# A context module with three recurrent scans: weights and images prepared differently, the image split moved into the scan's first blocks

## The reference

```
r, z = sigmoid(Wx_r x + Wh_r h), sigmoid(Wx_z x + Wh_z h)
n    = tanh(Wx_n x + r * (Wh_n h))
ctx  = (1 - z) * n + z * h
h    = tanh(conv1d(ctx, 3 taps) + bias)
```

## Time and profile before

| | before |
|---|---|
| median of 3 runs | 397.28 us |
| profiled execution, its own time | 396.7 us |
| its span | 395.0 us |
| PE / DVE / ACT / POOL busy | 323.7 / 316.5 / 273.0 / 16.6 us |
| mean granted TensorE clock | 0.969 |
| bytes read from HBM | 6.16 MB |

### The profile page before, as it was taken

One profiled execution on the slowest core, in us unless ns is written; L12 is line 12 of the kernel. 1 busy time (PEld: TensorE's weight loads), 2 busy tenths in 40 slices (PEclk: granted clock), 3 DMA queues, 4 the chain that ended last, 5 costly groups with the idle time before them and its releaser, 6 DMA issues.

```text
span 395.0 us, 7885 instructions
## 1 busy us (share of the span) xinstructions
PE 323.7 (82%) x2702; PEld 264.6 (67%) x2702; DVE 316.5 (80%) x750; ACT 273.0 (69%) x541; POOL 16.6 (4%) x26
## 2 busy tenths in 40 slices
PE   0101233487999999999999999999999999999995
PEld 0101112255888888888888888888888888885442
DVE  0663499969989989989989989889899899896532
ACT  6539896774777777777777777777777777775800
POOL 1072300000000000000000000000000000000000
PEclk9999968659999999999999999999999999999999
DMA  8700000000000000000000000000000000000544
GB/s 309 315 0 0 1 0 1 0 2 0 2 0 0 0 0 0 0 0 0 0 0 0 0 0 0 0 0 0 0 0 0 0 0 0 0 0 0 161 123 143
DMA packets 10199, 10.43 MB, mean 26 GB/s; under 512 B 465, under 2 KB 8785, under 8 KB 10193
## 3 DMA queue, kind: packets, MB, share of 16 engines
q1 hardware_dynamic: 10192, 10.36, 7.7%
HBM read 6.16 MB, written 4.19 MB: 26 GB/s over the span
## 4 chain that ended last, share of the span: by engine, by line
PE 76%; DVE 9%; ACT 7%; issue 3%; POOL 2%; DMA 1%; POOLq 0%
PE rz_bank L679 20%; PE conv_bank L679 15%; PE rz_bank L682 10%; PE n_bank L679 10%; PE conv_bank L682 8%; PE n_bank L682 5%; DVE x_rows L533 5%; ACT x_rows L371 2%; DVE x_rows L525 2%; PE rz_bank L766 1%; PE n_bank L770 1%; PE rz_bank L770 1%; PE n_bank L768 1%; PE rz_bank L768 1%; PE n_bank L766 1%
## 5 line engine op out<-in xcount | busy, mean ns | idle before, releaser
L679 PE MATMUL conv_bank<-ctx_store,w_parts 128*128 (+1 forms) x558 | 108.9, 276 | 16.0 <-ACT ctx_store L424 9.5
L679 PE MATMUL rz_bank<-x_rows,w_parts 128*128 (+1 forms) x384 | 81.1, 278 | 6.7 <-issue 6.7
L413 ACT ACTIVATE nval<-npre 128x256 f32<-128x256 f32 x93 | 38.7, 417 | 65.0 <-DVE npre L616 64.9
L679 PE MATMUL rz_bank<-h_parts,w_parts 128*128 128x256 f16 x372 | 77.4, 275 | 0.1
L401 ACT ACTIVATE rz<-rz_bank,descale 128x512 f32<-128x512 f32 x96 | 65.9, 687 | 15.1 <-PE rz_bank L679 7.0
L679 PEld LDWEIGHTS conv_bank<-ctx_store,w_parts 128*128 128x128 f16 x558 | 54.7, 98 | 30.1 <-ACT ctx_store L424 10.9
L604 DVE SCALAR_TENSOR_TENSOR npre<-n_bank,descale,rz 128x256 f32<-128x256 f32 x93 | 45.0, 484 | 27.7 <-ACT rz L401 27.6
L682 PE MATMUL conv_bank<-ctx_store,w_parts 128*128 (+1 forms) x279 | 67.1, 276 | 0.0
L682 PE MATMUL rz_bank<-x_rows,w_parts 128*128 (+1 forms) x192 | 53.5, 279 | 0.0
L418 ACT ACTIVATE hval<-conv_bank,biases,descale 128x256 f32<-128x256 f32 x93 | 51.4, 552 | 0.8 <-PE conv_bank L679 0.8
L679 PE MATMUL n_bank<-x_rows,w_parts 128*128 (+1 forms) x192 | 48.2, 277 | 0.0
(11 more groups left out here) (80 smaller groups left out, 450.9 us busy)
## 6 DMA issues: line engine op xcount, KB each, us to landing
x<-x_dram SPq DMA_DIRECT2D x8, 512.0 KB, 9.1
out_dram<-x_rows SPq DMA_DIRECT2D x8, 512.0 KB, 3.2
ctx_store<-weights_dram SPq DMA_DIRECT2D x3, 576.0 KB, 5.0
ctx_store<-weights_dram SPq DMA_DIRECT2D x1, 192.0 KB, 6.0
biases<-biases_dram SPq DMA_DIRECT2D x1, 2.0 KB, 11.5
```

Source lines behind the costliest of these rows:

```text
L679: last = nc.tensor.matmul(out, w_block(HI, k, n), parts(hi_or_lo), start=start, stop=stop and hi_or_lo == LO, skip_group_check=True)
```

## The change

It does the following.

- **Loads.** Weights of direction 0, then the eight images, then the other weights. As the images are now normalised in place in `x32`, the input is loaded a second time once all of it is split (SyncE waits for the last strip).
- **Weight scales.** The maximum over partitions is taken with two small PE products and a DVE maximum instead of POOL's, in two groups (direction 0 first). ACT scales and rounds in one instruction straight to HI; LO is made by DVE, in ten units of 384 elements, six of them (five with their HI in the first four blocks, the output's in block (3, 1)) inside the scan.
- **Statistics.** ACT takes images 2 and 5, DVE the other six. One group average for the mean and one for the variance of all eight images together. POOL's power gives the scale directly.
- **Normalising** is in place. First rows 0, 1, 30, 31 of each image (128 elements), then the last four columns (112), and the inner core (28 x 28) inside blocks (0, 1) to (1, 0).
- **Split in strips across images.** A strip takes a few rows or columns of all eight images in one instruction: HI by ACT, LO by DVE, which waits for that strip's HI. Only the first two rows (512 elements) are done before PE starts, the last two rows after them. 17 strips are in the blocks of `SPLIT_IN_BLOCK`, from (0, 0) to (9, 2). In elements: (0,0) 896; (1,0), (1,1), (1,2), (2,1), (2,2), (3,0) 448 each; (2,0) 512; (4,0), (4,2), (6,0), (6,2) 384 each; (5,1) 256; (7,2), (8,1), (9,0), (9,2) 320 each. A strip stands in a block where `rest_hi` and `rest_lo` stood: after `gates` on ACT and after `reset_hidden` on DVE. The order in which a strip is walked is image, row, column, as the access pattern says.
- **Steps 0 to 10** are written out (11 instead of 2).
- PE has 12, 4, 4 and 6 dummy products of 512 columns in the head instead of 8.

The core of the diff:

```diff
+SPLIT_IN_BLOCK = {
+    (0, 0): LAST_COLS,
+    (1, 0): Cells((2, 4), (0, W - 4)),
+    (1, 1): Cells((H - 4, H - 2), (0, W - 4)),
...
+    (9, 2): Cells((18, 20), (0, W - 12)),
+}
+        def all_images(ap, cells):
+            return ap[:, cells.rows, cells.cols, :].rearrange("p h w b -> p b h w")
...
-            for t in (0, 1):
+            for t in range(UNROLLED):
...
+            load_weights(0)
             for b in range(B):
                 sp.dma_start(x32[:, b, :, :], x_d[b, :, :, :]).then_inc(x_loaded[b], 16)
+            for k in (1, 2, COMB):
+                load_weights(k)
...
+            sp.wait_ge(x_lo_done, SPLITS)
+            for b in range(B):
+                sp.dma_start(x32[:, b, :, :], x_d[b, :, :, :]).then_inc(x_loaded[b], 16)
...
+            def x_hi(cells, normed):
+
+                act.wait_ge(x_normed, normed * (B - len(ACT_NORMED)))
+                act.wait_ge(x_normed_act, normed * len(ACT_NORMED))
+                nc.scalar.activation(all_images(x_rows[:, HI, :, :, :], cells),
+                                     x32[:, :, cells.rows, cells.cols], ACT.Copy).then_inc(x_hi_done, 1)
...
-                for b in REST_HI_IN_BLOCK.get((t, j), ()) if isinstance(t, int) else ():
-                    rest_hi(b)
+                if isinstance(t, int):
+                    for unit in UNITS_IN_BLOCK.get((t, j), ()):
+                        weights_hi(UNITS.index(unit))
+                    for b in CORE_ON_ACT.get((t, j), ()):
+                        normalise(b, core)
+                    if (t, j) in SPLIT_IN_BLOCK:
+                        x_hi(SPLIT_IN_BLOCK[t, j], 2 if t == 0 else 3)
...
+            def x_lo(cells):
+
+                lo_count[0] += 1
+                dve.wait_ge(x_hi_done, lo_count[0])
+                nc.vector.tensor_tensor(out=all_images(x_rows[:, LO, :, :, :], cells),
+                                        in0=x32[:, :, cells.rows, cells.cols],
+                                        in1=all_images(x_rows[:, HI, :, :, :], cells),
+                                        op=ALU.subtract).then_inc(x_lo_done, 1)
```

More of the change, by code:

```diff
@@ L231, in conv_scale, with edges, strip, core @@
         def conv_scale(k):
[L232 to L246, removed]
+            return descale[:, 2 * k + 1:2 * k + 2]
+        def edges(ap):
+            return ap.rearrange("p (g r) w -> p g (r w)", r=2)[:, 0:H // 2:H // 2 - 1, :]
+        def strip(ap):
+            return ap[:, LAST_COLS.rows, LAST_COLS.cols]
+        def core(ap):
+            return ap[:, LAST_COLS.rows, 0:LAST_COLS.cols.start]
+        def all_images(ap, cells):
+            return ap[:, cells.rows, cells.cols, :].rearrange("p h w b -> p b h w")
+        def unit_blocks(unit):
+            kind, *k = UNITS[unit].split()
+            if kind == "comb":
+                return COMB_SET, 0, DIRS
+            k = int(k[0])
+            first = DIRS + k * DIR_BLOCKS + GATES * ("in", "rec", "conv").index(kind)
+            return 2 * k + (kind == "conv"), first, first + GATES
+        def merged(ap):
+            return ap.rearrange("p n c -> p (n c)")
         block = ctx.enter_context(nc.Block())
@@ L296, in weights_lo @@
[L296 to L310, removed]
@@ L313, in _ @@
[L313 to L325, removed]
+            pool.wait_ge(var_eps, 1)
+            nc.gpsimd.tensor_tensor(out=x_scale[:], in0=gvar[:], in1=minus_half[:], op=ALU.pow) \
+                .then_inc(pow_done, 1)
@@ L331, in _, with moment, magnitude_sums @@
             nc.scalar.activation(first_sigmoid[:], minus_half[:, 0:1], ACT.Sigmoid)
-            for k in range(DIRS + 1):
+            moments = [0]
+            def moment(instruction):
+                moments[0] += 1
+                instruction.then_inc(act_moments, 1)
+                act.wait_ge(act_moments, moments[0])
+            def magnitude_sums(k):
                 act.wait_ge(w_loaded[k], 16)
@@ new lines, in weights_hi, with normalise @@
+            def weights_hi(unit):
+                n, lo, hi = unit_blocks(unit)
+                act.wait_ge(scale_done, 1 if n < SET_GROUPS[0][1] else 2)
+                nc.scalar.activation(w_parts[:, HI, lo:hi, :], w32[:, lo:hi, :], ACT.Copy,
+                                     scale=w_scale[:, n:n + 1]).then_inc(w_hi_done, 1)
+            def normalise(b, cells):
+                act.wait_ge(x_factor, 1)
+                nc.scalar.activation(cells(x32[:, b, :, :]), cells(x32[:, b, :, :]), ACT.Identity,
@@ L377, in _ @@
[L377 to L392, removed]
@@ L393, in _ @@
-            rest_hi(WHOLE_IMAGES)
+            def x_hi(cells, normed):
[3 more added lines that the diff above has]
+                                     x32[:, :, cells.rows, cells.cols], ACT.Copy).then_inc(x_hi_done, 1)
+            magnitude_sums(0)
+            image_moments(ACT_IMAGES[0])
+            for unit in range(3):
+                weights_hi(unit)
@@ L396, in _ @@
+            image_moments(ACT_IMAGES[1])
+            for k in (1, 2, COMB):
+                magnitude_sums(k)
+            for b in ACT_NORMED:
+                normalise(b, edges)
+            x_hi(FIRST_ROWS, 1)
+            x_hi(LAST_ROWS, 1)
+            for b in ACT_NORMED:
+                normalise(b, strip)
+            weights_hi(UNITS.index("in 1"))
             act.wait_ge(bias_loaded, 16)
@@ L450, in steps @@
                     hidden_hi(*before)
[L451 to L454 removed]
             gates(0, 0)
             blocks(act, steps)
+            for b in range(B):
+                act.wait_ge(x_loaded[b], 32)
             for c in range(CHUNKS):
@@ L549, in _ @@
+            dve_normed = [b for b in range(B) if b not in ACT_NORMED]
             image_stats(0)
-            weight_scales()
+            sets_peak(0)
             image_stats(1)
-            image_stats(2)
-            spread(0)
+            weight_scales(0)
             image_stats(3)
-            variance(0)
             image_stats(4)
-            factor(0)
-            shift(0)
-            image_stats(5)
+            weights_lo(0)
+            weights_lo(1)
             image_stats(6)
-            normalise(2)
@@ L562, in _ @@
[L562 removed]
             image_stats(7)
[L564 to L578 removed]
+            spread()
+            weights_lo(2)
+            variance()
@@ L580, in lines @@
+            shift()
+            for b in dve_normed:
+                normalise(b, edges)
+            sets_peak(1)
+            x_lo(FIRST_ROWS)
+            weight_scales(1)
+            x_lo(LAST_ROWS)
+            for b in dve_normed:
+                normalise(b, strip)
+            weights_lo(UNITS.index("in 1"))
             def lines(ap):
@@ L638, in steps @@
                 if exists(now[1]):
-                    for b in REST_LO_IN_BLOCK.get((t, j), ()) if isinstance(t, int) else ():
-                        rest_lo(b)
+                    if isinstance(t, int):
+                        for unit in UNITS_IN_BLOCK.get((t, j), ()):
+                            weights_lo(UNITS.index(unit))
+                        for b in CORE_ON_DVE.get((t, j), ()):
+                            normalise(b, core)
+                        if (t, j) in SPLIT_IN_BLOCK:
+                            x_lo(SPLIT_IN_BLOCK[t, j])
                     context_lo(*now)
@@ new lines, in warm @@
+            def warm(products):
+                for _ in range(products):
+                    nc.tensor.matmul(rz_bank[2][:], w_block(HI, 0, 0),
+                                     merged(w_parts[:, HI, DIRS:DIRS + OUT_COLS // C, :]),
+                                     start=True, stop=True, skip_group_check=True)
+            pe.wait_ge(pool_built, 6)
+            turn_sums(0)
+            spread_peaks(0)
+            pe.wait_ge(w_hi_done, 2)
+            warm(FRONT_WARM)
+            pe.wait_ge(aggr_done, B - len(ACT_IMAGES))
```

305 lines of the change are left out of this document (160 added, 145 removed).

## The result

The changed kernel takes 429.9 us (median of 4, 429.33 to 431.29), the kernel before beside it 396.7: ratio 1.084, interval 1.079 to 1.088. The profiled execution took 430.4 us with a span of 428.5.

The account below looks back on a forecast made before the run. PE was taken to bound the steady scan, not the head. Head and first blocks gain 29.3 us, gates 6 to 32 cost 62.7 more, so 396.7 + 33.4 = 430; range 388 to 456 holds 0.8.

Parts of the forecast that it names:

- The head and first blocks: Start to gates 6: first scan product at 28 us, gates 6 at 64.6 against 93.95, ahead by 29.3 us.
- HI, LO and context_lo in a row: Blocks with a strip: x_hi 0.59 after gates, handoff 0.04, x_lo, context_lo 0.27 later, next gates 1.53 later.
- The size of a strip block: Gates to gates with a strip of n elements: 3.30 + 0.00849 n us; fifteen blocks together 98.9.
- The clock: Gates 6 to 32: PE's idle waits lower its clock, near 0.6 in blocks (1, 1) to (3, 0); 7 us, ends 0 and 30.
- Eleven blocks without a strip: Gates 6 to 32: 11 x 2.95 = 32.5 us, plus 1.0 for the output's weights in (3, 1).
- Priced at nothing: Second load of x, 0 to 5 us if it disturbs the scan; nine more written-out steps, 0, up to 10 if late.
- HI hides: Rival, chance 0.10: in strip blocks ACT gets ahead, so x_hi is done when x_lo comes up; 395 us.
- Cheap: Rival, chance 0.16: a strip element costs 1 ns on either engine, as without a step; 369 us.

Follow-up runs that it names:

- e2: The changed kernel with ACT writing HI of each strip one strip earlier, so LO in the same block finds it done; 399.7 us.
- e4: The changed kernel with all cores normalised and all strips split ahead of the scan, none left in a block; 389.0 us.
- e1: The changed kernel with three of PE's waits for strips, in blocks (1,2), (2,0) and (8,0), asking for one strip less; 418.6 us.
- e9: e1 plus dummy PE products in convolutions behind strips, none for step 0's strip, PE's two waits in old order where there are no dummies; 413.3 us.
- e11: The changed kernel with strips and cores ahead of the scan, walked row, column, image, and 4 steps written out; 364.1 us, against 364.5 with 11 steps.
- e3: The changed kernel with each strip walked row, column, image instead of image, row, column; 376.9 us.
- e10: e1 with only PE's two waits ahead of each convolution reordered, hidden value first and context_hi last, no dummies; 423.4 us.

## Why the prediction was right

430 was predicted and 429.9 measured. The mechanism was right: a shorter head, then blocks that pay for HI and LO one behind the other. The closeness is luck: one term was 9.9 us too large, and another, of 10.7 us, was missing.

- **The head and first blocks.** Gates 1, 3 and 6 within 1.1 us of the forecast. The product of group averages, the power and the edge rows came in the order given; DVE finished its statistics at 16.97 rather than 17.5.
- **HI, LO and context_lo in a row.** The steps of 0.59 and 0.27 us, read from the trace before, are there again, and the handoff of 0.04 is 0.03. e2 shows that the row is the cost, e4 that the place is.
- **The size of a strip block, mis-sized.** Forecast 3.30 + 0.00849 n; where the clock did not lengthen the block 448 took 6.46 and 320 took 5.33: 2.5 + 0.0088 n. Of 0.64 too much at 448, 0.35 is the two instructions (the line through 256 and 720 elements of overlapping ones gave 2.39 and 2.29, measured 2.18 and 2.15), and 0.28 the 1.53 from context_lo to gates, read from one block whose hidden_lo took 0.74 where others take 0.42; here it is 1.25. Over fifteen strips, with the blocks as measured (5 x 6.46 + 7.0 + 4 x 5.91 + 4.75 + 4 x 5.33 = 89), 9.9 too much.
- **PE's waits for strips, missed.** The prediction said of PE in a strip block that it "has only the 9 input products and 6 of the convolution to go on with". In three blocks it had not even these. The waits were in the diff; I had not laid PE's block beside the block before of the other engines. e1 shows the cost: from gates 6 to gates 32 it took 128.3 in place of 139.1, 10.7 less.
- **The clock, right in size, not in depth.** Forecast 7; e9 shows at least 5, and about 6 with what the dummies cost. But it did not stay near 0.6 in blocks (1, 1) to (3, 0), as the prediction had it: the mean there was 0.78, with 0.67 in (1, 1) and 1.00 in (2, 1).
- **Eleven blocks without a strip** took 34.7 together, forecast 33.5 without the clock. At full clock they make 33.0 (ten of 2.95 and (3, 1) with 3.45).
- **Priced at nothing.** The written-out steps cost nothing (e11). The second load moves 292 GB/s from 207 to 215, and the block there, gates to gates, takes 2.95.

From gates 6 to gates 32 the forecast was 98.9 + 33.5 + 7 = 139.4. Measured are 89.0 for blocks with a strip and 33.0 for those without, both where the clock did not lengthen them, and 10.7 for the waits, and the 6.4 that are left of 139.06 are about what e9 puts on the clock. Past gates 32, block (10, 0) took 3.78 in place of 2.95, which the forecast did not have either; in e1 it took 2.96.

Of the rivals, *HI hides* was priced at 395, and e2, which makes its condition true for all fifteen strips of these blocks but not for (0, 0) and (1, 0), took 399.7. *Cheap* was priced at 369, and the walk that makes strips cheap took 376.9 (e3). That e3 with the relaxed waits gives 369.5 is again two errors that cancel: the price had 1 ns an element, where 1.7 were measured, and did not have the waits. In the changed kernel neither condition held.

The Trainium skill's page "SBUF — State Buffer" (section "Door 1: The DMA port swizzle", box on cachelines) says that SBUF has 16-byte lines and that each access that crosses to a new line pays. It took weight from *cheap*. The runs agree for the write: walking the strips so that eight writes fall in one line took 2.8 ns from an element. For the read they show a smaller price: at a step of 4096 bytes each element lies in a line of its own, and reading and writing together took 1.7 ns.

## What to carry to other kernels

Work put into the blocks of a tight pipeline is hidden only if the block's chain of waits, not its engines' busy share, has room. Here ACT was idle for 26% of the steady blocks, and yet a strip of 448 elements, with 4.3 us of HI and LO, made a block 3.5 us longer. Two engines that handle the same piece one after the other in each block pay twice. Let the first run one piece ahead (30 us here), or do it all beforehand, where they work side by side (41 us). Where the engines go through the blocks at an offset, count what a wait asks for by what is read next, not by the number of the block (11 us). And before deciding where to put an expensive instruction, look at which side of it is stepped: turning the walk so that the write was contiguous was worth 53 us, more than any placement.

## What the runs showed of the hardware

- A write of 16-bit elements with a step of 16 bytes took 4.3 to 4.5 ns an element on ACT and on DVE alike in the changed kernel, and 448 elements took 2.21 and 2.16 us when both did it at once (e2), against 2.18 and 2.15 in turn. With the writes contiguous and the 32-bit read at a step of 4096 bytes, it was 1.7 (e3).
- PE has two waits ahead of each convolution, one for a hidden value, done over 1 us before, and one for context_hi, which ends about 0.1 us before the product starts. With context_hi waited for last, the steady block took 2.985 us (e10), with it first 2.947 (e1). Why, the runs do not show.
- Filling PE's waits with products that nobody reads kept the granted clock at 1.00 in place of 0.90 and shortened the stretch from gates 7 to gates 32 by 5 us in 122 (e9 against e1), though HI and LO on ACT and DVE hold 43% of the chain there in e1.
